# A gated linear recurrence rewritten on sigmoids and logarithms, with GpSimd taken out of it

## The reference

```
proj = x @ W1 + b1;  hidden, forget, input = split(proj, 3)
diff = softplus(-forget) - softplus(-input)
log_coeffs     = -softplus(diff)
log_val_coeffs = -softplus(-diff)
log_g(v) = log(relu(v) + 0.5) if v >= 0 else -softplus(-v)
log_h = cumulative log-sum-exp of these over time, from log_g(init_h)
s = exp(log_h) @ W2 + b2
```

## Time and profile before

| | us |
|---|---|
| runs (3) | 4411.47, 4409.26, 4401.57; median 4409.26 |
| span of the profiled execution, first to last instruction | 4402.1 |
| shared sweep | to about 1163 |
| recurrence, first gate matmul to last output matmul | 1179.5 to 2776 |
| routed sweep | from 2781 to the end |
| PE busy over the span | 4061.1 (92%) |
| DVE busy | 2581.3 (59%) |
| ACT busy | 1813.5 (41%) |
| POOL busy | 1453.2 (33%) |

### The profile page before, as it was taken

One profiled execution on the slowest core, in us unless ns is written; L12 is line 12 of the kernel. 1 busy time (PEld: TensorE's weight loads), 2 busy tenths in 40 slices (PEclk: granted clock), 3 DMA queues, 4 the chain that ended last, 5 costly groups with the idle time before them and its releaser, 6 DMA issues. The chain is left out here.

```text
span 4402.1 us, 56358 instructions
## 1 busy us (share of the span) xinstructions
PE 4061.1 (92%) x17851; PEld 3246.7 (74%) x17852; DVE 2581.3 (59%) x3328; ACT 1813.5 (41%) x2581; POOL 1453.2 (33%) x1245
## 2 busy tenths in 40 slices
PE   7999999999788999999999999699999999999997
PEld 6888888888666777777777777577777777777776
DVE  4323232322488888888888888555556565655564
ACT  3222222222255555555555555333334333433432
POOL 2010110101055222222222222444445455554553
PEclk9999999999899999999999999899999999999999
DMA  4121211211120100000110000545455455555552
GB/s 162 60 86 67 76 71 71 83 60 77 48 61 25 40 29 29 29 29 29 39 48 29 29 29 10 217 174 183 172 181 198 165 199 203 201 204 183 181 200 86
DMA packets 197719, 447.12 MB, mean 102 GB/s; under 512 B 19705, under 2 KB 36281, under 8 KB 193794
## 3 DMA queue, kind: packets, MB, share of 16 engines
q1 hardware_dynamic: 165170, 346.24, 22.0%
q0 software_dynamic: 32464, 99.94, 6.3%
HBM read 345.38 MB, written 104.68 MB: 102 GB/s over the span
## 5 line engine op out<-in xcount | busy, mean ns | idle before, releaser
L85 PE MATMUL gate<-xT,w_hi 128*128 128x512 f32 x1536 | 601.3, 391 | 8.2 <-DVE w_lo L95 8.2
L86 PE MATMUL gate<-xT,w_hi 128*128 128x512 f32 x1536 | 600.1, 391 | 0.0
L87 PE MATMUL gate<-xT,w_lo 128*128 128x512 f32 x1536 | 599.6, 390 | 0.0
L1259 DVE TENSOR_TENSOR wlo<-raw,whi 128x2048 fp32r<-128x2048 f32 x128 | 488.2, 3814 | 23.0 <-ACT whi L1255 23.0
L521 DVE TENSOR_TENSOR h_act<-h_act,psU 128x512 f32<-128x512 f32 x128 | 88.0, 687 | 688.6 <-PE psU L87 688.5
L1466 PE MATMUL tY<-whi,thT 128*128 128x512 f32 x1264 | 431.9, 412 | 31.3 <-DVE thT L1399 27.4
L1255 ACT ACTIVATE whi<-raw 128x2048 fp32r<-128x2048 f32 x192 | 367.5, 1915 | 42.4 <-PE tU L87 22.3
L1100 PE MATMUL rpsY<-w_hi,rhT 128*128 128x512 f32 x512 | 222.5, 434 | 134.8 <-ACT rhT L899 134.8
L85 PEld LDWEIGHTS gate<-xT,w_hi 128*128 128x128 f32 x1536 | 290.0, 189 | 71.3 <-issue 5.8
L86 PEld LDWEIGHTS gate<-xT,w_hi 128*128 128x128 f32 x1536 | 289.9, 189 | 61.7
L87 PEld LDWEIGHTS gate<-xT,w_lo 128*128 128x128 f32 x1536 | 289.8, 189 | 61.6
(11 more groups left out here) (205 smaller groups left out, 9727.7 us busy)
## 6 DMA issues: line engine op xcount, KB each, us to landing
raw<-in_L_ffn_routed_gate_w SPq DMA_DIRECT2D x64, 1024.0 KB, 5.4
raw<-in_L_ffn_routed_up_w SPq DMA_DIRECT2D x64, 1024.0 KB, 5.0
raw<-in_L_ffn_routed_down_w SPq DMA_DIRECT2D x64, 1024.0 KB
xT_dram<-xT SPq DMA_DIRECT2D x16, 2048.0 KB, 6.3
xT<-xT_dram SPq DMA_DIRECT2D x14, 2048.0 KB, 7.8
x_in<-in_L_attn_x SPq DMA_DIRECT2D x16, 1024.0 KB, 6.0
xs_dram<-x_in SPq DMA_DIRECT2D x16, 1024.0 KB, 4.4
ss_dram<-y_sb SPq DMA_DIRECT2D x64, 256.0 KB, 2.0
```

The source lines that it names most:

```text
L85: pe.matmul(out, w[0], x[0], start=start, stop=False)
L86: pe.matmul(out, w[0], x[1], start=False, stop=False)
L87: return pe.matmul(out, w[1], x[0], start=False, stop=stop)
L1259: eng.tensor_tensor(wlo[q][:], raw[q][:], whi[q][:], ALU.subtract).then_inc(wlo_done[q], 1)
```

## The change

It rewrites the pointwise part. With `lf = min(f, ln(sig(f) + 1e-30))`, and `li` likewise, the coefficients are `b = sig(li - lf)` and `a = sig(lf - li)`, and `g = max(h + 0.5, sig(h))`. ACT now takes three sigmoids from PSUM, two logarithms and two sigmoids of the difference; sigmoid and logarithm are in different tables. POOL keeps only the copy of the last column and the indirect DMAs. PE makes the gates in the order forget, input, hidden, and waits for a bank of the unit before by `logf_done`, `logi_done` and `g_done`. The raw weights have two places, `y` and a new tile `spare`; ACT and DVE split slice n + 2 in unit n. `b2row` has its own tile and is loaded behind slice 0. The initial state takes one sigmoid in place of exp, ln, exp.

```
-        raw1 = y[:, 0:3]...;  raw2 = y[:, 3]
+        raw1 = [r[:, 0:3]... for r in (y, spare)]
+        raw2 = [r[:, 3] for r in (y, spare)]
 @ sync
+            def load_weights(kb):
+                j = kb % 2
+                at_least(sp, w2_lo, kb - 1)
+                for kk in range(KD):
+                    sp.dma_start(raw1[j][:, kk], w1_part(w1v, kb)[:, kk]).then_inc(w1_loaded[j], 16)
+                sp.dma_start(raw2[j], w2v[:, kb, :]).then_inc(w2_loaded[j], 16)
+            load_weights(0)
+            sp.dma_start(b2row[:], b2.rearrange("(a n) -> a n", a=1)).then_inc(small, 16)
 @ gpsimd, body
-                    pool.tensor_tensor(dn[:], pa[:], qb[:], ALU.add).then_inc(d_done, 1)
-                    pool.wait_ge(r_done, U + 1)
-                    pool.tensor_tensor(qb[:], qb[:], dn[:], ALU.mult).then_inc(c_done, 1)
+                    tail(U, kb)
 @ scalar
+            act.preload_act_table_set(SIGMOID_SET)
+            act.activation(i1[:], i0[:], ACT.Sigmoid).then_inc(init_done, 1)
+            act.wait_ge(rows_set, 2)
+            hi(0)
+            hi(1)
 body (the eleven activations of lines 915 to 943 go)
+                    act.wait_ge(f_mm, U + 1)
+                    act.wait_ge(df_done, U)
+                    act.activation(lf[:], bank(n, 0)[:], ACT.Sigmoid, bias=bias(GF, kb)).then_inc(sf_done, 1)
                     if not (first and n == 0):
                         split(U - 1)
+                    act.wait_ge(i_mm, U + 1)
+                    act.activation(li[:], bank(n, 1)[:], ACT.Sigmoid, bias=bias(GI, kb)).then_inc(si_done, 1)
+                    act.wait_ge(sf_done, U + 1)
+                    act.activation(lf[:], lf[:], ACT.Ln, bias=tiny[:, 0:1]).then_inc(lnf_done, 1)
+                    act.wait_ge(si_done, U + 1)
+                    act.activation(li[:], li[:], ACT.Ln, bias=tiny[:, 0:1]).then_inc(lni_done, 1)
+                    act.wait_ge(h_mm, U + 1)
+                    act.wait_ge(bg_done, U)
+                    act.activation(gh[:], bank(n, 2)[:], ACT.Sigmoid, bias=bias(GH, kb)).then_inc(sh_done, 1)
+                    act.wait_ge(df_done, U + 1)
+                    act.wait_ge(scan_done, U)
+                    act.activation(qb[:], df[:], ACT.Sigmoid).then_inc(b_done, 1)
+                    act.activation(pa[:], df[:], ACT.Sigmoid, scale=-1.0).then_inc(a_done, 1)
                     if first and n + 2 < NB:
-                        hi(n + 2 if n else 1)
+                        hi(n + 2)
 @ vector
             lo(0)
+            dve.wait_ge(b2_mm, 1)
+            dve.tensor_copy(b2all[:], psY[0][:]).then_inc(consts, 1)
+            dve.wait_ge(consts, 3)
+            lo(1)
 body (the nine operations of lines 1034 to 1070 go)
                     if lag:
                         scan(U - 1, (n - 1) % UPS)
                         split(U - 1)
+                    dve.wait_ge(lnf_done, U + 1)
+                    dve.scalar_tensor_tensor(lf[:], bank(n, 0)[:], bias(GF, kb), lf[:], ALU.add, ALU.min)
+                    dve.wait_ge(lni_done, U + 1)
+                    dve.scalar_tensor_tensor(li[:], bank(n, 1)[:], bias(GI, kb), li[:], ALU.add, ALU.min)
+                    dve.wait_ge(a_done, U)
+                    dve.wait_ge(b_done, U)
+                    dve.tensor_tensor(df[:], li[:], lf[:], ALU.subtract).then_inc(df_done, 1)
+                    dve.wait_ge(sh_done, U + 1)
+                    dve.scalar_tensor_tensor(gh[:], bank(n, 2)[:], bh5[:, kb:kb + 1], gh[:], ALU.add, ALU.max)
                     if first and n + 2 < NB:
-                        lo(n + 2 if n else 1)
+                        lo(n + 2)
+                    if kb == 0 and lag:
                         output(seq * CPS + n // NB - 1)
 @ tensor
+            pe.wait_ge(consts, 3)
 body
+                    if not (first and n < 2):
+                        pe.wait_ge(g_done, U - 1)
+                    gate_mm(n, 0, GF, j, f_mm)
+                    pe.wait_ge(logf_done, U)
+                    gate_mm(n, 1, GI, j, i_mm)
+                    pe.wait_ge(logi_done, U)
+                    gate_mm(n, 2, GH, j, h_mm)
```

More of the change, by code:

```diff
@@ L748, in recurrence_sweep @@
         one_row = k.sb("one_row", [1, P])
-        one = k.sb("one", [P, 1])
+        tiny = k.sb("tiny", [P, 1])
         start = k.sb("start", [P, NB])
@@ L755, in recurrence_sweep @@
         diff = k.sb("diff", [1, 2, L - 1])
[L756 to L761, removed]
+        i1 = k.sb("init_sigmoid", [P, NB])
+        lf = k.sb("log_f", [P, CHUNK])
+        li = k.sb("log_i", [P, CHUNK])
+        gh = k.sb("g_h", [P, CHUNK])
+        df = k.sb("log_ratio", [P, CHUNK])
         pa = k.sb("pa", [P, CHUNK])
         qb = k.sb("qb", [P, CHUNK])
[L764 to L770, removed]
         hs = k.sb("hs", [P, CHUNK])
@@ L795, in recurrence_sweep @@
         settled = k.sem("settled2")
-        w1_loaded, w2_loaded = k.sem("w1_loaded"), k.sem("w2_loaded")
+        w1_loaded = [k.sem(f"w1_loaded{j}") for j in range(2)]
+        w2_loaded = [k.sem(f"w2_loaded{j}") for j in range(2)]
         w1_hi, w1_lo, w2_hi, w2_lo = (k.sem(n) for n in ("w1_hi", "w1_lo", "w2_hi", "w2_lo"))
@@ L800, in bias, with bank @@
             return b1s[:, g * NB + kb:g * NB + kb + 1]
+        def bank(n, g):
+            return gate[(3 * n + g) % 4]
         def sequences(eng, body):
@@ L907, in _ @@
             hi(0)
+            hi(1)
             def body(u0, seq, first):
-                act.preload_act_table_set("natural_log_exp_and_others")
+                act.preload_act_table_set(SIGMOID_SET)
                 for n in range(UPS):
                     U, kb = u0 + n, n % NB
[L913 to L916, removed]
+                    act.wait_ge(f_mm, U + 1)
+                    act.wait_ge(df_done, U)
+                    act.activation(lf[:], bank(n, 0)[:], ACT.Sigmoid, bias=bias(GF, kb)).then_inc(sf_done, 1)
@@ L935, in body @@
[L935 to L942, removed]
@@ new lines, in body @@
+                    dve.wait_ge(lnf_done, U + 1)
+                    dve.scalar_tensor_tensor(lf[:], bank(n, 0)[:], bias(GF, kb), lf[:], ALU.add, ALU.min)\
+                        .then_inc(logf_done, 1)
+                    dve.wait_ge(lni_done, U + 1)
+                    dve.scalar_tensor_tensor(li[:], bank(n, 1)[:], bias(GI, kb), li[:], ALU.add, ALU.min)\
+                        .then_inc(logi_done, 1)
+                    dve.wait_ge(logf_done, U + 1)
+                    dve.wait_ge(logi_done, U + 1)
@@ L1056, in body @@
+                    dve.wait_ge(a_done, U)
+                    dve.wait_ge(b_done, U)
+                    dve.tensor_tensor(df[:], li[:], lf[:], ALU.subtract).then_inc(df_done, 1)
+                    dve.wait_ge(sh_done, U + 1)
+                    dve.scalar_tensor_tensor(gh[:], bank(n, 2)[:], bh5[:, kb:kb + 1], gh[:], ALU.add, ALU.max)\
+                        .then_inc(g_done, 1)
                     if first and n + 2 < NB:
-                        lo(n + 2 if n else 1)
-                    if kb == 0 and not (first and n == 0):
+                        lo(n + 2)
@@ L1067, in body @@
-                    dve.wait_ge(sig_done, U + 1)
-                    dve.wait_ge(hp_done, U + 1)
-                    dve.wait_ge(b_done, U)
-                    dve.tensor_tensor(gg[:], hp[:], sd[:], ALU.max).then_inc(g_done, 1)
-                    if first and n == 0:
-                        lo(2)
                     if first:
@@ L1108, in outputs, with gate_mm @@
                 mm.then_inc(out_mm, 1)
+            def gate_mm(n, g, third, j, done):
+                kb = n % NB
+                cols = slice(third * z.DIN + kb * P, third * z.DIN + (kb + 1) * P)
+                for kk in range(KD):
+                    mm = matmul_pairs(pe, bank(n, g)[:], (w1[0][:, kk, cols], w1[1][:, kk, cols]),
+                                      (xT[j][:, 0, kk, :], xT[j][:, 1, kk, :]), kk == 0, kk == KD - 1)
+                mm.then_inc(done, 1)
             def body(u0, seq, first):
@@ L1116, in body @@
                         pe.wait_ge(w1_lo, n + 1)
-                    for g, third, done, freed in ((0, GI, i_mm, None), (1, GF, f_mm, isb_done), (2, GH, h_mm, du_done)):
-                        bank = gate[(3 * n + g) % 4]
-                        if g > 0:
-                            pe.wait_ge(freed, U)
-                        elif not (first and n < 2):
-                            pe.wait_ge(hm_done, U - 1)
-                            pe.wait_ge(hp_done, U - 1)
-                        cols = slice(third * z.DIN + kb * P, third * z.DIN + (kb + 1) * P)
-                        for kk in range(KD):
-                            mm = matmul_pairs(pe, bank[:], (w1[0][:, kk, cols], w1[1][:, kk, cols]),
-                                              (xT[j][:, 0, kk, :], xT[j][:, 1, kk, :]), kk == 0, kk == KD - 1)
-                        mm.then_inc(done, 1)
+                    if not (first and n < 2):
[5 more added lines that the diff above has]
```

(1 more changed line is left out.)

147 lines of the change are left out of this document (36 added, 111 removed).

## The result

The changed kernel takes 4231.1 us (median of 4, 4225.34 to 4234.65) against 4406.3 (4 runs of before beside it). The ratio is 0.9605, 95% interval 0.959 to 0.962. The forecast was 4236 us, with a range of 4212 to 4290.

The account below looks back on a forecast made before the run. The recurrence was held to be bound by a pointwise chain ending 1.0 us late per unit. Gains of 37.6 (first sequence), 127.8 (111 units) and 7.8 (end), 173 us, gave span 4229, forecast 4236 us, range 4212 to 4290.

Parts of the forecast that it names:

- What bounds the unit: Recurrence: outputs wait for ScalarE's rounding of rhT, so a late pointwise chain costs 1.0 us of each 11.94 us unit.
- The new chain: Each unit, from its first gate matmul: scan ends at 13.8, rounding at 15.2, needed at 19.1; slack 3.9 us.
- The second limit: ScalarE's own round, including standing for the scan: 9.3 us with hand-overs against 10.94, leaving 1.6 us.
- Unit of 10.94: TensorE's own stream sets the unit: 10.94 us where it was 11.94; 111 units gain 127.8 us.
- The rival of 0.233: TensorE's back-to-back matmul step is 0.233 us: 37 us more, 4273 us; chance 0.07.
- First sequence: Units before the second sequence: first gate at 1177.3, 192.6 us long, second sequence starts 37.6 us earlier, at 1369.9.
- the ring of the staged units: Units 1 to 6, weights still being split: a round through ScalarE and VectorE binds at 13.8 us with hand-overs.
- a ring that isn't met: Units 1 to 6 of the first sequence: if the scan is served in time, 15 us gained.
- Two raw places: Weight loading in the first sequence: next slice is loaded, splitting runs two slices early, nothing there waits for a DMA.
- End: Last unit's gates to last output matmul: 18.6 us where it was 26.4, gain 7.8 us.
- Switches: ScalarE: two table loads a unit, 1.283 us each; one switch 1.31 us from end to start.
- The doubled cost: Rival: a table switch costs 2.57 us, ScalarE's round 11.9 us, time 4362 us; chance 0.07, skill's drain included.

Follow-up runs that it names:

- contention-only run: Kernel before without GpSimd's second product (qb unscaled, so not the recurrence's result), GpSimd's sum kept: 4273.7 us, ratio 0.9708.
- reordered run: Kernel after with VectorE's low parts of the weights and count of places moved behind the scan in the first sequence: 4215.7 us, ratio 0.9569.
- The first experiment: Kernel before with both GpSimd products issued by VectorE, all else unchanged: 4415.1 us, ratio to before 1.0021.
- six loads: Kernel after with two one-column exponentials a unit, forcing four more table loads: 4659.2 us, ratio to before 1.0586.

## Why the prediction was right, step by step

- *What bounds the unit.* Right: a chain that ended 1.0 us late. The contention-only run put a size on its cause, 1.09 us. What the prediction described is the latency to the outputs; the run with GpSimd out shows that for the kernel before it was a ring of 11.94 us that bound.
- *The new chain.* Right, within 0.2 us at each step: the scan ends 2.9 us into the next unit's gates (13.8 forecast less 10.94). The second limit, a round of 9.3, is a ring of 8.8, and 2.2 us are spare, not 1.6. I had added records end to end, while successive operations of an engine overlap by some 0.1 us each.
- *Unit of 10.94.* It is 10.99: mis-sized by 0.05. Output matmuls with their two hops take 3.03 us (0.233 to the first, 2.80 for the rest) where I had 2.77 + 0.22, and the gate step is 0.2276 where it was 0.227. Over 111 units 6 us, the whole miss in that term. The rival of 0.233 is out. Of the range 0.222 to 0.228 that I took from the counts of the shared sweep, only the lower end follows from the row (200 / 898 = 0.223).
- *First sequence.* Forecast 37.6, found 42.4: first gate 1.6 us earlier, the ring of the staged units 13.19 where I summed 13.8, again the overlaps. The 1.6 us may be chance: in the runs whose staging is the same the first gate came at 1174.8 to 1176.8. The mechanism was right, as the reordered run shows by removing it. The 15 us that I gave for a ring that isn't met are 17.7 by their own terms (14.3 + 5 x 13.8 - 6 x 10.94); the reordered run measured 15.4.
- *Two raw places.* I gave them no term of their own and wrote only that nothing waits for a DMA; one place does as well.
- *End.* 19.2 us, forecast as 18.6: the last 12 matmuls took 4.53 us where I had 4.
- *The sum.* The three terms came out 4.8 us above, 5.9 below and 0.5 below the forecast, so the recurrence gained 171.6 us against 173. That it is this near is in part luck. The span came out at 4223.6 against 4229, because the 7 us of the routed sweep were not forecast. The 7.2 us kept between the span and the median are luck too. They came out as 7.5, but a run's time on record is only 1.6 to 2.0 us above its own span; the rest is that both profiled executions were among the fastest of their kernel.
- *Switches.* 1.283 us in all 256 records and 1.30 from start to start in the timelines shown, forced ones too. The doubled cost and the Trainium skill's 2.66 us ("ScalarE: Activation LUTs", section "What ACT_TABLE_LOAD costs") are refuted for this kernel. The load of 1283 ns that the page gives is exact; the drain of 1380 ns that it adds is not seen.
- *Where I was wrong* is outside the sum: I took GpSimd's exit for a gain that could be had alone. The first experiment cost 12 us where I expected 85 less.

## What to carry to other kernels

Where two engines pass work to and fro in each unit, sum the ring once round, start to start, and compare it with the bound engine's stream; only what shortens the ring pays, and only down to the stream. Taking an engine out is worth the contention it caused only if its work leaves the ring too; moved onto an engine in the ring it costs as much as it frees. Work that is due later (here weights for two units ahead) belongs in a wait of the in-order engine, not in front of the operation that the others wait for.

## What the runs showed of the hardware

- A 128x512 product of two SBUF operands on VectorE took 1.66 us on average beside GpSimd's product and 0.686 with that product gone. GpSimd's own took 1.758 beside VectorE and 1.289 with VectorE waiting: both pay. Not every operation beside it does: in the unit of the earlier trace rows `pa * dn`, which began 0.04 us ahead of GpSimd's product, took 0.69, and `gg`, which began after it, 1.78.

```profile
L880 POOL TENSOR_TENSOR qb<-qb,dn 128x512 f32<-128x512 f32 x128 | 225.1, 1758 | 244.9 <-ACT dn L941 244.9
...
2705.73 0.69 DVE L1066 TENSOR_TENSOR pa<-pa,dn 128x512 f32<-128x512 f32 x1 [0.44 <-ACT dn L941]
```

- Repeated explicit table loads of one set left no record of their own; a load appears where the next function needs another table.
- With a stall of some 3 us of TensorE in each unit (six loads) the mean granted clock in the stretch fell to 0.94, where it was 1.00 in the kernel before with 1.0 us a unit.

```profile
1600.00:1800.00 200.00, 167.59 (x672) 132.44 (x672) 83.35 (x109) 187.07 (x227) 2.59 (x14) 0.94 0.09 32
```
